# Grouped attention: the values' product in f16 halves, three per product, with probabilities turned three units late

## The reference

```python
q = (h @ wq).reshape(B, S, NHEADS, HEAD_DIM)      # 32 heads of 64
k = (h @ wk).reshape(B, S, KVHEADS, HEAD_DIM)     # 8
v = (h @ wv).reshape(B, S, KVHEADS, HEAD_DIM)
q, k = _rope(q, k)
...
scores = where(causal, q k^T / sqrt(64), -1e30)
attn = softmax(scores, -1)
o = einsum('bhqk,bkhd->bqhd', attn, v)
x = x + o @ wo
```

## Time and profile before

| | us |
|---|---|
| median of 3 runs | 799.43 |
| lowest and highest | 795.02, 800.53 |
| the profiled execution | 799.23 |
| its span, first to last instruction | 797.4 |
| mean granted clock of TensorE | 0.917 |
| busy: PE, PEld | 632.0, 441.5 |
| busy: DVE, ACT, POOL | 557.4, 431.2, 463.4 |

### The profile page before, as it was taken

The page is one execution under the profiler, slowest core; times in us unless marked ns, Lnnn a source line. Parts: engine busy times, 40 slices in busy tenths (PEclk is TensorE's granted clock), DMA queues, the critical chain, the costliest instruction groups (busy, mean ns, idle before and its releaser), DMA issues.

```text
span 797.4 us, 16336 instructions
## 1 busy us (share of the span) xinstructions
PE 632.0 (79%) x5656; PEld 441.5 (55%) x5656; DVE 557.4 (70%) x1420; ACT 431.2 (54%) x1213; POOL 463.4 (58%) x424
## 2 busy tenths in 40 slices
PE   0247999468888844689999999999887789999970
PEld 0124667246566533367777777677675436666640
DVE  5999558868878976856677577677656765555445
ACT  4823532059768820456576666666654217777640
POOL 1051654248977942269698788768532336777750
PEclk9778896789999976989999999999999979999995
DMA  9500130127536530024042332422500913333428
GB/s 299 189 1 1 49 110 1 53 79 221 168 118 207 158 121 1 0 54 80 15 89 46 93 55 42 67 28 50 177 15 8 401 47 96 105 108 109 103 84 263
DMA packets 83466, 77.99 MB, mean 98 GB/s; under 512 B 49408, under 2 KB 75776, under 8 KB 82880
## 3 DMA queue, kind: packets, MB, share of 16 engines
q1 hardware_dynamic: 78880, 64.33, 28.0%
q0 software_dynamic: 4512, 12.71, 5.5%
HBM read 47.46 MB, written 18.55 MB: 83 GB/s over the span
## 4 chain that ended last, share of the span: by engine, by line
PE 52%; DVE 24%; ACT 7%; POOL 7%; issue 6%; DMA 2%; SPq 1%; POOLq 0%; ACTq 0%; DVEq 0%
PE ps L1800 10%; PE ps L2093 8%; PE ps L2015 5%; PE ps L1999 5%; PE ps L1982 5%; PE ps L2116 4%; ACT arena L974 2%; PE ps L1765 2%; PE ps L1857 2%; DVE arena L1496 2%; PE ps L1743 2%; POOL arena L832 2%; DVE tiny L1489 2%; PE ps L1724 2%; ACT arena L1059 1%
## 5 line engine op out<-in xcount | busy, mean ns | idle before, releaser
L1059 ACT ACTIVATE arena<-ps,tiny 128x128 f32<-128x128 f32 (+1 forms) x256 | 104.2, 419 | 53.6 <-DVE tiny L1489 53.6
L832 POOL TENSOR_TENSOR arena<-arena,tiny 128x512 f32<-128x512 f32 x64 | 93.9, 1467 | 62.9 <-DVE tiny L1500 62.6
L1496 DVE COPY arena<-ps 128x512 f32<-128x512 f32 x64 | 44.3, 691 | 75.3 <-PE ps L1982 75.3
L2093 PE MATMUL ps<-arena 128*128 (+1 forms) x282 | 68.7, 380 | 1.0 <-DVE arena L1640 0.5
L1800 PE MATMUL ps<-arena,xt_hi 128*128 128x512 f16 (+1 forms) x224 | 64.2, 372 | 3.6 <-DVE xt_lo L1278 3.0
L867 POOL DMA_INDIRECT arena<-h_store,arena x47 | 46.0, 979 | 33.5 <-DVE arena L1619 19.5
L1999 PE MATMUL ps<-arena 128*64 128x128 f32 x768 | 56.1, 280 | 11.3 <-DVE arena L1504 11.3
L1489 DVE TENSOR_REDUCE tiny<-ps 128x4 f32<-128x512 f32 x64 | 60.9, 952 | 1.3 <-PE ps L1967 0.9
L1999 PEld LDWEIGHTS ps<-arena 128*64 128x64 f32 x768 | 41.4, 136 | 32.3 <-issue 23.1
L1633 DVE SCALAR_TENSOR_TENSOR ps<-ps,arena 128x256 f32<-128x256 f32 x47 | 20.3, 433 | 55.4 <-ACT arena L1111 55.4
L1965 PE MATMUL ps<-arena 128*128 128x128 f16 (+1 forms) x256 | 58.5, 247 | 0.2 <-ACT arena L1038 0.2
(11 more groups left out here) (295 smaller groups left out, 1738.4 us busy)
## 6 DMA issues: line engine op xcount, KB each, us to landing
e_store<-arena SPq DMA_DIRECT2D x13, 768.0 KB, 4.3
arena<-e_store SPq DMA_DIRECT2D x13, 768.0 KB, 9.4
work<-w_dram SPq DMA_DIRECT2D x27, 256.0 KB, 4.6
xn<-w_dram SPq DMA_DIRECT2D x21, 256.0 KB, 4.7
arena<-w_gate_up_t_dram SPq DMA_DIRECT2D x2, 1024.0 KB, 8.9
arena<-wq_dram SPq DMA_DIRECT2D x2, 1024.0 KB, 7.4
arena<-wo_dram SPq DMA_DIRECT2D x2, 1024.0 KB, 5.8
work<-y_store SPq DMA_DIRECT2D x8, 256.0 KB, 5.2
```

The costliest lines, as they stand in the source:

```text
L832: nc.gpsimd.tensor_tensor(p, p, arec[:, u % 4, :].unsqueeze(2).broadcast_to([P, GH, L]), ALU.mult)\
L1059: nc.scalar.activation(ap_[u % 3][:, h, 0:L], head_scores(u, h), ACT.Exp, bias=anm[:, u % 4, h:h + 1], accum_out=asum[:, u % 4, h:h + 1]). ...
L1496: nc.vector.tensor_copy(apt[:, u % 2, 0, :], ps[:, 3, :]).then_inc(a_pt, 1)
L2093: last = mm(ps[:, 2 + i % 2, :], xg[:, i % 2, x_half * KB + k, :], weights(hidden_weights(slot, w_half, k), i), start=(n == 0), stop=(n == 5))
```

## The change

Probabilities and values are held as two f16 halves. `pt_hi` on ACT copies both banks at once to f16, scaled by `WS` (64); `pt_lo` on DVE subtracts that from the same banks and writes the rest; likewise `value_lo` on DVE after `token_hi` for values. `a_values` makes three f16 products of 256 columns for each key block and half (hi hi, hi lo, lo hi) where four f32 products of 128 columns stood for each key block; `output_hi` and `output_lo` take out the factor. Turning and all behind it come a unit later: `a_turn(i-3)`, `pt_hi(i-3)`, `pt_lo(i-3)`, `a_values(i-3)`, `output_hi(i-4)`, `output_lo(i-4)`, `out_projection(i-4)`; `ap_` gets a fourth buffer and `normalise` follows it. On DVE `pt_lo` now stands behind `row_reciprocal`, and `value_lo` of i-1 at the head of the turn.

```diff
--- before.py
+++ after.py
@@ -271,11 +271,14 @@
 
 
         q2 = c5([QRING, 8, 2, HD], F16)
-        apt = c5([2, TB, GH * P], F32)
+        apt_hi = c5([2, TB, GH * P], F16)
+        apt_lo = c5([2, TB, GH * P], F16)
         ka, kb2 = ([c5([NG, 2, HD], F16), t[:, 0:2, :, :].rearrange("p b k n -> p (b k n)")
                     .rearrange("p (g m d) -> p g m d", m=2, d=HD)] for t in (ct_hi, ct_lo))
         anm, asum, arec = (tiny[:, i * 16:(i + 1) * 16].rearrange("p (u h) -> p u h", u=4) for i in range(3))
-        av = [carver(37888, 38912)([TB, NG * HD], F32), c5([TB, NG * HD], F32)]
+        av_halves = [carver(37888, 38912)([2, TB, NG * HD], F16), c5([2, TB, NG * HD], F16)]
+        ap_.append(c5([GH, S], F32))
+        av_hi, av_lo = ([v[:, half, :, :] for v in av_halves] for half in range(2))
 
 
         e_raw = [t[:, 0:EW // D, :].rearrange("p t d -> p (t d)") for t in (xn, work2)]
@@ -1015,8 +1019,10 @@
                 b, c, t, _ = SIDE[n]
                 if c == VAL:
                     act.wait_ge(proj, n + 1)
-                    nc.scalar.activation(av[b % 2][:, t, :], ps[:, SIDE_BANK[n], :], ACT.Copy, scale=1.0 / WS)\
-                        .then_inc(v_ready, 1)
+                    if b >= 2:
+                        act.wait_ge(a_o, (b - 1) * AU)
+                    nc.scalar.activation(av_hi[b % 2][:, t, :], ps[:, SIDE_BANK[n], :], ACT.Copy, scale=1.0 / WS)\
+                        .then_inc(v_hi_ready, 1)
                     return
                 m = ROPES.index(n)
                 y = yb[:, m % 2, :].rearrange("p (h d) -> p h d", d=HD)
@@ -1037,26 +1043,29 @@
                 act.wait_ge(tok_transposed, r + 1)
                 nc.scalar.activation(turn_target(r), heads_bank(TURNS[r][3]), ACT.Copy).then_inc(qt_act, 1)
 
-            def pt_second(u):
+            def pt_hi(u):
+                k = u % TB + 1
                 act.wait_ge(a_pt_trans, u + 1)
                 if u >= 2:
                     act.wait_ge(a_o, u - 1)
-                nc.scalar.activation(apt[:, u % 2, 1, :], ps[:, 4, :], ACT.Copy).then_inc(a_pt2, 1)
+                nc.scalar.activation(apt_hi[:, u % 2, 0:k, :].rearrange("p k q -> p (k q)"),
+                                     ps[:, 3:3 + k, :].rearrange("p k q -> p (k q)"), ACT.Copy, scale=WS)\
+                    .then_inc(a_pt_hi, 1)
 
             def output_hi(u):
                 act.wait_ge(a_o, u + 1)
                 if u >= 4:
                     act.wait_ge(wo_out, u - 3)
-                nc.scalar.activation(ot_hi[:, u % 4, :, :].rearrange("p o q -> p (o q)"), ps[:, 5, 0:2 * P], ACT.Copy)\
-                    .then_inc(ot_hi_ready, 1)
+                nc.scalar.activation(ot_hi[:, u % 4, :, :].rearrange("p o q -> p (o q)"), ps[:, 5, 0:2 * P], ACT.Copy,
+                                     scale=1.0 / WS).then_inc(ot_hi_ready, 1)
 
             def exponentials(u):
                 L = (u % TB + 1) * P
                 act.wait_ge(a_max, u + 1)
-                if u >= 3:
-                    act.wait_ge(a_pt_trans, u - 2)
+                if u >= 4:
+                    act.wait_ge(a_pt_trans, u - 3)
                 for h in range(GH):
-                    nc.scalar.activation(ap_[u % 3][:, h, 0:L], head_scores(u, h), ACT.Exp, bias=anm[:, u % 4, h:h + 1],
+                    nc.scalar.activation(ap_[u % 4][:, h, 0:L], head_scores(u, h), ACT.Exp, bias=anm[:, u % 4, h:h + 1],
                                          accum_out=asum[:, u % 4, h:h + 1]).then_inc(a_exp, 1)
 
             for n in sides_at(-1)[:6]:
@@ -1066,11 +1075,11 @@
                     turned_tokens(r)
             for n in sides_at(-1)[6:]:
                 token_hi(n)
-            for i in range(UNITS + 3):
-                if i >= 3:
-                    output_hi(i - 3)
-                if 2 <= i < UNITS + 2 and i % 2:
-                    pt_second(i - 2)
+            for i in range(UNITS + 4):
+                if i >= 4:
+                    output_hi(i - 4)
+                if 3 <= i < UNITS + 3:
+                    pt_hi(i - 3)
                 for n in sides_at(i - 1) if i else []:
                     token_hi(n)
                 if i < UNITS:
@@ -1489,11 +1498,19 @@
                 nc.vector.tensor_reduce(anm[:, u % 4, :].rearrange("p (m h) -> p m h", m=u % TB + 1), scores,
                                         AX.X, ALU.max, negate=True).then_inc(a_max, 1)
 
-            def pt_first(u):
-                vec.wait_ge(a_pt_trans, u + 1)
-                if u >= 2:
-                    vec.wait_ge(a_o, u - 1)
-                nc.vector.tensor_copy(apt[:, u % 2, 0, :], ps[:, 3, :]).then_inc(a_pt, 1)
+            def pt_lo(u):
+                k = u % TB + 1
+                vec.wait_ge(a_pt_hi, u + 1)
+                flat = "p k q -> p (k q)"
+                nc.vector.scalar_tensor_tensor(apt_lo[:, u % 2, 0:k, :].rearrange(flat), ps[:, 3:3 + k, :].rearrange(flat),
+                                               WS, apt_hi[:, u % 2, 0:k, :].rearrange(flat), ALU.mult, ALU.subtract)\
+                    .then_inc(a_pt, 1)
+
+            def value_lo(n):
+                b, _, t, _ = SIDE[n]
+                vec.wait_ge(v_hi_ready, vals_to(n))
+                nc.vector.scalar_tensor_tensor(av_lo[b % 2][:, t, :], ps[:, SIDE_BANK[n], :], 1.0 / WS,
+                                               av_hi[b % 2][:, t, :], ALU.mult, ALU.subtract).then_inc(v_ready, 1)
 
             def row_reciprocal(u):
                 vec.wait_ge(a_exp, GH * (u + 1))
@@ -1501,9 +1518,9 @@
 
             def output_lo(u):
                 vec.wait_ge(ot_hi_ready, u + 1)
-                nc.vector.tensor_tensor(ot_lo[:, u % 4, :, :].rearrange("p o q -> p (o q)"), ps[:, 5, 0:2 * P],
-                                        ot_hi[:, u % 4, :, :].rearrange("p o q -> p (o q)"), ALU.subtract)\
-                    .then_inc(a_o_read, 1)
+                nc.vector.scalar_tensor_tensor(ot_lo[:, u % 4, :, :].rearrange("p o q -> p (o q)"), ps[:, 5, 0:2 * P],
+                                               1.0 / WS, ot_hi[:, u % 4, :, :].rearrange("p o q -> p (o q)"),
+                                               ALU.mult, ALU.subtract).then_inc(a_o_read, 1)
 
             def add_attention(b):
                 vec.wait_ge(wo_out, (b + 1) * AU)
@@ -1520,16 +1537,22 @@
             for r in turns_at(-1):
                 if TURNS[r][4] == "vec":
                     turned_tokens(r)
-            for i in range(UNITS + 3):
-                if 2 <= i < UNITS + 2:
-                    pt_first(i - 2)
+            for n in sides_at(-1):
+                if n in VALS:
+                    value_lo(n)
+            for i in range(UNITS + 4):
+                for n in sides_at(i - 1) if i else []:
+                    if n in VALS:
+                        value_lo(n)
                 if 1 <= i <= UNITS:
                     row_reciprocal(i - 1)
-                if i >= 3:
-                    output_lo(i - 3)
+                if 3 <= i < UNITS + 3:
+                    pt_lo(i - 3)
+                if i >= 4:
+                    output_lo(i - 4)
                 if i < UNITS:
                     score_max(i)
-                if i > AU and i % AU == 3:
+                if i > AU and i % AU == 4:
                     add_attention(i // AU - 1)
                 for n in sides_at(i):
                     if n in ROPES:
@@ -1973,13 +1996,11 @@
                 if u:
                     pe.wait_ge(a_pt, u)
                 if t:
-                    if u > 1:
-                        pe.wait_ge(a_pt2, u // 2)
                     past = [r for r in range(FIRST_TURNS) if TURNS[r][3] == 4]
                     pe.wait_ge(*read_out(past[-1]))
                 for k in range(t + 1):
                     for h in range(GH):
-                        last = nc.tensor.transpose(ps[:, 3 + k, h * P:(h + 1) * P], ap_[u % 3][:, h, k * P:(k + 1) * P],
+                        last = nc.tensor.transpose(ps[:, 3 + k, h * P:(h + 1) * P], ap_[u % 4][:, h, k * P:(k + 1) * P],
                                                    ident[:, :])
                 last.then_inc(a_pt_trans, 1)
 
@@ -1988,17 +2009,15 @@
                 if g == 0:
                     pe.wait_ge(v_ready, b * TB + t + 1)
                 pe.wait_ge(a_pt, u + 1)
-                if t:
-                    pe.wait_ge(a_pt2, u // 2 + 1)
                 if u:
                     pe.wait_ge(a_o_read, u)
-                for pair in range(GH // 2):
-                    for k in range(t + 1):
+                cols = slice(g * HD, (g + 1) * HD)
+                for k in range(t + 1):
+                    for n, (v, p) in enumerate(((av_hi, apt_hi), (av_hi, apt_lo), (av_lo, apt_hi))):
+                        pairs = p[:, u % 2, k, :].rearrange("p (a half q) -> p a half q", half=2, q=P)
                         for half in range(2):
-                            h = pair * 2 + half
```

(24 more changed lines are left out.)

## The result

The changed kernel takes **871.37 us** (median of 4 runs, 867.46 to 873.02) against 797.52 for the kernel before, timed beside it: 1.0927 times as long, 95% interval 1.0885 to 1.0969. The profiled execution, the fastest of the four, has a span of 865.4 us (797.4 before), a mean granted clock of 0.912 and PE busy 73% of the span. The forecast was 869, range 853 to 893.

A forecast was written before the change was run, and what follows sets the result against it. The prediction took a serial DVE and ACT chain to bound the changed loop, 9.84 us a pair against 8.7 or 7.66. Loop +53.3, end +6.8 and clock +10 make 70 on 799.23: 869 us, range 853 to 893.

The forecast's parts named there:

- The ring: Attention loop: DVE and ACT hand work back and forth, pt_hi and pt_lo join in series; 9.84 us a pair of units.
- The lag hides nothing: Attention loop: the lag of three doesn't help, as pt_hi and pt_lo stand ahead of the next exponentials and maximum.
- value_lo: Six value projections in the loop: DVE waits for token_hi, then makes value_lo; 1.15 us each, 6.9 in all.
- Ahead of S0: Before unit 0's score maximum starts: its scores wait for two value_lo, 1.2 to 1.9 us late, 1.6 taken.
- The end: From the start of unit 63's score maximum to the last addition: 17.7 us against 10.96, +6.8.
- The clock: PE in the loop: long standstills mostly bring 1.2 GHz; 10 us added, bounds 0 and 46.
- long gaps: PE standing still about 3 us: five pairs from unit 54 on, three even units with value_lo; eight at 1.7 us, a quarter spared.
- no slack at t=0: PE's values, out_projection and turn after a one-block unit's maximum starts: done at 2.31 us, ACT needs them at 2.38.
- PE stays the bound: Rival, attention loop: the DVE and ACT chain is hidden, a pair under 8.7 us; 797 us, no change. Chance 0.05.
- No lower clock: Whole kernel: a granted clock of 1.00 to the end was a sign against the forecast, giving 859 us.
- The lower rival (853): Rival: the lower clock never comes and handovers are 0.2 us a pair shorter; 853 us. Chance 0.09, with values to 863.

The follow-up runs named there:

- short_lo: Changed kernel with pt_lo writing 16 columns in place of 512 or 1024, its product taking the high half again: 823.44 us, 1.0357 of the kernel before.
- tokens_last: Changed kernel, outputs a unit later, DVE: output_lo, value_lo, maximum, pt_lo last; ACT: value copies before pt_hi, key/query token_hi behind exponentials: 805.09 us, 1.0133 of the kernel before.
- halves_lag2: Changed kernel with a lag of two units in place of three: 862.79 us, 1.0822 of the kernel before.
- values_later_only: Changed kernel with values, out_projection, output_hi and output_lo one unit later, DVE's order kept: 866.42 us, 1.0914 of the kernel before.
- lag_only: Kernel before, f32 copies and products kept, with only the lag of three and the fourth buffer: 795.62 us, 1.0011 of the kernel before.
- kept_busy: Changed kernel with useless matmuls in PE's gaps from unit 54 on: 858.04 us, 1.0799 of the kernel before.
- pool_beside_add: Changed kernel with one useless POOL product behind unit 63's normalisation, to lie beside DVE's 1536-column addition: 870.69 us in one run.

## Why the prediction was right, and which terms were not

- **The ring.** Forecast 9.84 us a pair, measured 9.82, and no step of it off by more than 0.04. The operation that the trace of before didn't have in this place, pt_lo, was priced by L1278 and took 0.69 (0.684 there). Place, not amount, was the right thing to ask for: short_lo takes both away together and shows the price of the link, tokens_last keeps all of the amount and gets 64 us back.
- **The lag hides nothing**, as said of the changed kernel: halves_lag2 and values_later_only. With f32 products it hides 3.3 us of the loop (lag_only).
- **value_lo.** Forecast 6 times 1.15, measured: a step with value_lo is 7.01 long (maxima at 384.17 and 391.18), its like without 5.87, so 1.14. Ahead of S0 forecast 1.6, measured 1.8.
- **Terms missing in the loop.** The first three steps took 11.64 in place of 10.4, 1.2 more, while the queues fill. add_attention costs 0.39 each at units 21, 37 and 53, where DVE stands in the ring with it: 1.2. Unit 4 costs 0.3. Thirty pairs came to 0.6 less. Together S0 to S63 gained 53.8 without the clock, where 51.7 were forecast.
- **The end.** Forecast 17.7 at full clock (its terms add up to 17.8), measured 17.65 (kept_busy), but one term of it stood for another. I put L1538 at 3.1 on the path. It took 1.75 and is off the path: in the changed kernel DVE waits 2.35 us for ACT's pt_hi behind it. What stands in its place is PE's work behind output_lo(60), values, out_projection and turn, then pt_hi: 2.94 from 660.68 to 663.62 in kept_busy. That two such terms agree is luck. I had taken the duration of the earlier trace rows without looking at what POOL did beside it.
- **The clock.** Forecast 10 us, all in the loop, from six of eight long gaps at 1.7 each. The size held (9.1, and 13.4 in pool_beside_add's one execution), the place did not, and that makes the size luck in part. The prediction counted three value units among the long gaps, at about 3.0 us. There PE's projection waits for value_lo and stands between turn and values, and the gap ahead of it is 2.26 us (first row below); in this execution no lower clock came of it. Of the five others the step paid at S55, S59 and S63, with 1.5, 1.2 and 2.2 us, and two paid nothing (second row: a gap of 3.04, and values at their usual length). The end, which I charged with nothing, paid 4.45.

```profile
389.80 0.60 PE L1823 MATMUL ps<-arena,xt_hi 128*128 128x512 f16 x2 [2.26 <-DVE arena L1512]
...
624.61 0.84 PE L2019 MATMUL ps<-arena 128*64 128x256 f16 x12 [3.04 <-DVE arena L1521]
```

PE's values, out_projection and turn of the step to S63 show what the clock does. Kernel after, PE's timeline, then busy times and granted clock (0.50) of this stretch, columns as in the earlier trace rows:

```profile
655.27 1.49 PE L2019 MATMUL ps<-arena 128*64 128x256 f16 x12 [3.05 <-DVE arena L1521]
656.70 1.46 PE L2034 MATMUL ps<-arena 128*128 128x256 f16 x6
657.95 1.06 PE L2003 MATMUL ps<-ident,arena 128*128 128x128 f32 x4
```

```profile
655.27:659.01 3.74, 3.74 (x23) 2.92 (x24) 0.63 (x2) 1.78 (x9) 1.04 (x1) 0.50 0.00 0
```

Behind a gap of 3.05 us the values take 1.49 where at 401.23 they took 0.85, out_projection 1.46 in place of 0.83, the turn 1.06 in place of 0.60. This path had no slack at t=0 in the forecast (2.31 of 2.38 us), and so it passes straight into S63.

- **PE stays the bound** (797) fell: PE busy 55.30 of 70. The saving on the products is real, 0.33 us a pair forecast and a little more measured (twelve f16 matmuls in 0.85 us, where sixteen f32 took 1.09, and six in 0.52, where eight took 0.66), but lies off the path. In tokens_last, where PE binds again beside the projections, it doesn't show over lag_only either: four units take 16.56 us in tokens_last and 16.55 in lag_only. What is saved goes into PE's waits ahead of the turn, 0.49 and 0.16 us in every four units. In the first of them pt_lo of the unit before, for which the turn waits in PE's code too, ended 0.10 us before the turn starts; the profile credits this wait to nobody, so that pt_lo is its cause is likely, not shown.

```profile
454.03 0.66 DVE L1510 SCALAR_TENSOR_TENSOR arena<-ps,arena 128x512 f16<-128x512 f32 x1
...
454.79 1.06 PE L2008 MATMUL ps<-ident,arena 128*128 128x128 f32 x8 [0.49 <-issue]
...
459.18 0.63 PE L2008 MATMUL ps<-ident,arena 128*128 128x128 f32 x4 [0.16 <-DVE arena L1510]
```

- **No lower clock.** For a clock of 1.00 to the end the prediction had 859, 60 us more than before. kept_busy, with its clock held up, took 62.7 more than the kernel before, timed beside it. The lower rival (853) also wanted shorter handovers, and these aren't shorter.
- **Readings on which the sum didn't hang.** Beside projections pairs before took 8.80 and 7.75 us in turn, 8.28 on average, and not 8.7: two projections stand in half of the pairs and not in three quarters. So PE would have stayed the bound only with a chain under 8.3. An f16 matmul of 256 columns comes to 0.112 us by the prediction's own division and not 0.109, and its 0.27 stands in none of the rows named.

## What to carry to other kernels

Where engines with in-order queues hand work to each other and back, follow the ring and add its links from rows; a link put into it costs its full length, whatever the busy shares say. A larger lag doesn't take the link out as long as the queues keep their order (9.82 to 9.87 us a pair at the three lags tried), and a new order may need the larger lag. Before an instruction is moved forward in such a queue, ask what it waits for itself, not only who waits behind it: twice here a new ring, longer than expected, came out of that. Splitting a result on one engine and its remainder on another makes two independent copies into two links in series; it needs a place in both queues where neither is waited for.

## What the runs showed of the hardware

DVE's addition of two f32 operands in SBUF, 1536 columns, took 1.75 us with POOL idle, 2.04 with 0.42 us of a POOL product beside it, 2.95 with 1.34 us and 3.15 with 1.53 us. POOL's product had started first each time, and the addition ended 1.61 to 1.62 us behind its end. Whether POOL would be the one to wait where DVE starts first, no run here shows. The Trainium skill, GPSIMD Engine Reference, "Specifications", has the SBUF interfaces shared with VectorE, with contention for instructions with two SBUF inputs; the rows agree. pt_lo, with one operand in PSUM and one in SBUF, didn't change: of 1024 columns it took 1.22 at 677.37 with POOL idle and 1.23 at 409.35, where POOL's product of 408.73 to 410.62 lay beside all of it.

The same gap of PE was followed by the lower clock at one time and not at another. Of the five gaps of 3.05 us from unit 54 on, three were in the changed kernel's execution, and all five in pool_beside_add's (3.05 to 3.34 us there), which spent 5 us more in the same loop. Of the three gaps of 2.3 us at the value units, none was in the one and one in the other (at 551.34, granted clock 0.54 in the next 3.7 us).
